# Query stacks loaded in 16 pieces of 512 bytes, from a scratch whose rows have gaps

## What is computed

```
x = x + xattn(layernorm(x), ctx, ctx)         # x, ctx: 128 x 64 x 128
    q = (x @ Wq.T + bq), k = (ctx @ Wk.T + bk), v = (ctx @ Wv.T + bv)   # 16 heads of 8
    scores = q k^T / sqrt(8); attn = softmax(scores); out = (attn v) @ Wo.T + bo
x = x + ffn(layernorm(x))
    so, si = softmax(bottleneck(x))           # two sets of 128 scores a token
    top 32 of so gate (x @ weight), top 32 of si gate x before "@ weight"
    + bias
```

## Time and profile before

| | |
|---|---|
| median of 3 runs | 524.53 us (522.14 to 526.05) |
| the profiled execution, its own time | 522.13 us |
| span of the profiled execution | 520.3 us |
| busy in the span: PE, DVE, ACT, POOL | 414.4, 408.7, 391.4, 363.5 us |
| DMA packets, bytes | 138970, 53.02 MB |
| chain that ended last: SP's queue, DMA | 27%, 7% of the span |
| first phase | to about 290 us |

### The profile page before, as it was taken

How to read it: one execution, slowest core, us unless ns; L and a number is a source line. 1 busy time by engine, 2 the same in 40 slices (tenths; PEclk the granted TensorE clock), 3 DMA queues, 4 the chain that set the end, 5 groups by cost and what they waited for, 6 DMA issues and landing times.

```text
span 520.3 us, 16344 instructions
## 1 busy us (share of the span) xinstructions
PE 414.4 (80%) x5516; PEld 314.0 (60%) x5516; DVE 408.7 (79%) x1940; ACT 391.4 (75%) x1061; POOL 363.5 (70%) x515
## 2 busy tenths in 40 slices
PE   3457999989999989999989564987787877777754
PEld 1125787868877858887777242765564645555543
DVE  7554478766777766767875359999999999999997
ACT  3414677867787858887667488899989898899893
POOL 7356667776777767876311023699989898999896
PEclk9997799988999999999999855578879698788687
DMA  5788788788788787788810000000000000000001
GB/s 159 157 211 196 159 197 196 197 204 195 172 183 184 191 195 176 161 185 182 178 47 7 1 0 2 1 21 23 21 22 37 12 36 22 21 21 22 23 21 40
DMA packets 138970, 53.02 MB, mean 102 GB/s; under 512 B 105146, under 2 KB 131195, under 8 KB 137339
## 3 DMA queue, kind: packets, MB, share of 16 engines
q1 hardware_dynamic: 136712, 51.47, 41.2%
q10 hardware_dynamic: 2176, 0.52, 0.5%
HBM read 34.67 MB, written 16.78 MB: 99 GB/s over the span
## 4 chain that ended last, share of the span: by engine, by line
DVE 37%; SPq 27%; PE 18%; DMA 7%; issue 4%; ACT 4%; POOL 2%; DVEq 0%; ACTq 0%; POOLq 0%
SPq L300 23%; DVE kst L1040 17%; DVE tops L1033 16%; DMA k_scratch<-k_parts 4%; PE ps_pv L360 4%; DMA qst<-q_scratch 3%; PE ps_col L345 2%; SPq L285 2%; PE ps_row L389 2%; PE ps_mix L375 1%; PE ps_proj L437 1%; SPq L247 1%; PE ps_proj L415 1%; PE ps_turn L430 1%; PE ps_mix L604 1%
## 5 line engine op out<-in xcount | busy, mean ns | idle before, releaser
L892 DVE TENSOR_REDUCE m<-ps_row 128x8 f32<-128x512 f32 x128 | 82.3, 686 | 57.1 <-PE ps_row L389 56.9
L650 ACT ACTIVATE pT<-ps_col 128x512 f32<-128x512 f32 x128 | 68.7, 589 | 29.1 <-PE ps_col L345 28.9
L1033 DVE MAX8 tops<-kst 128x8 f32<-128x128 f32 x384 | 78.1, 268 | 0.0
L360 PE MATMUL ps_pv<-vx,pT 128*64 128x18 f32 x2048 | 73.3, 214 | 0.0
L360 PEld LDWEIGHTS ps_pv<-vx,pT 128*64 128x64 f32 x2048 | 66.9, 141 | 7.1 <-issue 4.5
L1040 DVE MATCH_REPLACE8 kst<-tops,kst 128x128 f32<-128x128 f32 x264 | 69.0, 266 | 0.0
L389 PE MATMUL ps_row<-kst,qst 96*64 96x128 bf16 x1024 | 42.7, 228 | 7.8 <-DMA qst<-q_scratch 7.7
L345 PEld LDWEIGHTS ps_col<-qst,kst 100*128 100x128 bf16 x1024 | 35.0, 100 | 22.8 <-issue 11.9
L345 PE MATMUL ps_col<-qst,kst 100*128 100x64 bf16 x1024 | 42.8, 197 | 5.9 <-DMA qst<-mT 5.7
L553 PE MATMUL ps_proj<-wf_sb,x2T 128*128 128x128 f32 x128 | 25.6, 362 | 26.2 <-ACT x2T L821 26.2
L389 PEld LDWEIGHTS ps_row<-kst,qst 96*64 96x64 bf16 x1024 | 33.5, 116 | 11.8 <-DMA qst<-q_scratch 9.9
(11 more groups left out here) (156 smaller groups left out, 1213.3 us busy)
## 6 DMA issues: line engine op xcount, KB each, us to landing
k_scratch<-k_parts SPq DMA_DIRECT2D x32, 192.0 KB, 3.0
q_scratch<-q_parts SPq DMA_DIRECT2D x32, 192.0 KB, 3.1
kst<-k_scratch SPq DMA_DIRECT2D x32, 192.0 KB
qst<-q_scratch SPq DMA_DIRECT2D x32, 192.0 KB
xr<-in_x_dram SPq DMA_DIRECT2D x16, 256.0 KB, 4.3
cT<-in_ctxT_dram SPq DMA_DIRECT2D x16, 256.0 KB, 3.6
kst<-k_scratch SPq DMA_DIRECT2D x32, 128.0 KB
qst<-q_scratch SPq DMA_DIRECT2D x32, 128.0 KB
```

The source lines that it names most:

```text
L360: mm = pe.matmul(pv_flat[pp * SEQ:(pp + 1) * SEQ, h * 2 * VW:(h + 1) * 2 * VW], pT[:, 2 * j + pp, hh, :], vx[s][:, 2 * hp + pp, h, :], sta ...
L650: act.activation(pT[:, b % PT_RING, :, :], ps_col[b % 2][:, :, :], ACT.Exp, scale=SCALE).then_inc(act_exp, 1)
L892: dve.tensor_reduce(m32[:, b // 4, :, 4 * j:4 * j + 4].rearrange("q a h -> q h a"), ps_row[b % 2][:, :, :, :], AX.X, ALU.max).then_inc(dve ...
L1033: ins = dve.max(tops[g % 2][:, n, 8 * rnd:8 * rnd + 8], source(g, rnd, n))
```

## The change

`q_scratch` gets rows of 288 instead of 256 elements (GAP = 32, 64 bytes that nobody reads), so the 16 heads of a row no longer touch: they lie 576 bytes apart. The write to it fills the first 256 of the 288. The queries' stack is read as `(n i) h t`, of which the first 256 elements of `t` are taken, so each row of 8192 bytes in `qst` is filled by 16 pieces of 512 bytes. The number of DMAs, their order, their rows, their bytes, their waits and their semaphores are unchanged, and the keys' scratch and stack keep their shapes (the keys' source is only written in another way). No other engine's program changes.

```diff
+GAP = 32
...
-        q_scratch = [nc.dram_tensor(f"q_scratch{s}", (2, PARTS, 128, HALF), BF16).ap() for s in range(2)]
+        q_scratch = [nc.dram_tensor(f"q_scratch{s}", (2, PARTS, 128, HALF + GAP), BF16).ap() for s in range(2)]
...
                 for a in range(2):
-                    sp.dma_start(scratch[s][a].rearrange("n c t -> c n t"),
+                    sp.dma_start(scratch[s][a, :, :, 0:HALF].rearrange("n c t -> c n t"),
                                  parts[:, :, a * HALF:(a + 1) * HALF]).then_inc(done[s], 16)
...
-                        src = scratch[s][a, first:first + n].rearrange("n (i h) t -> (n i) (h t)", h=HEADS)
+                        src = scratch[s][a, first:first + n].rearrange("n (i h) t -> (n i) h t", h=HEADS)
                         rows = spread(a, n)
                         dst = (kst[d][rows, :, :, a, :].rearrange("r h p m -> r (h p) m") if to_keys
-                               else qst[d][rows, :, :].rearrange("r h t -> r (h t)"))
+                               else qst[d][rows, :, :])
                         if to_keys:
-                            src = src.rearrange("r (x m) -> r x m", m=SEQ)
+                            src = src.rearrange("r h (p m) -> r (h p) m", m=SEQ)
+                        else:
+                            src = src[:, :, 0:HALF]
                         sp.dma_start(dst, src).then_inc(moved[d], 16)
```

## The result

The changed kernel takes 528.68 us in the median of 20 runs (524.9 to 533.4), the kernel before 525.36 us in 20 runs beside it (518.24 to 531.24). The medians differ by 3.3 us (0.6%), the means by 3.7 us (0.7%, with a 95% interval of roughly 2 to 5.5 us). The ratio used from here on, 1.0096 with a 95% interval of 1.0067 to 1.0124 (5.0 us, 3.5 to 6.5), compares only executions within 1.5% of their kernel's fastest, which drops 8 of the 20 of the kernel before, whose fastest is a lone 518.24, and 2 of the 20 changed ones. So the changed kernel is slower, and by 3 to 5 us; these runs don't settle it more closely.

The account below looks back on a forecast made before the run. SP's queue was taken to bound most of the first phase, with PE close behind. Issue time of 3.1 us plus landings of 0.2 us gave 3.3 us, so 527.8 us on a median of 524.53, range 521 to 539 us.

Parts of the forecast that it names:

- Issue time: SP's six queries' stack issues: 45 ns more each, 0.27 us a group, 3.1 us in all.
- The signs that were named: Queries' issues with a minimum near 560 and a median near 665 ns; some 23000 more packets of 512 bytes.
- The upper end of 120 ns: Most that a queries' issue on SP might gain, from the keys' 737 ns against 617; 8.4 us in all.
- 11.6 from the chain: Groups of the 16 in which a longer queries' stack costs time: 120 us on the chain over 10.3 us a group.
- Transfer: Queries' rows on the DMA engines: 0.44 to 0.456 us each, 0.016 more, hidden behind the issue.
- Landing: PE's wait for a group's last queries' transfer: some four landings on the chain at 0.05 us each, 0.2 us.
- Pieces outlast their issue: Above 33 ns a piece, the queries' load sets the pace instead of its issue: 14.7 us more, 539.3 us; chance 0.18.
- Pieces hold up the next issue: SP's issue behind a queries' DMA of 384 pieces is held up: 7 us more, 534.8 us; chance 0.17.
- Smaller packets share better: Shorter packets let `qst<-mT` between them, halving PE's waits: 520.9 us, or 517.8 without the issue surcharge; chance 0.1.
- The rival that the PE slack swallows the change: SP's surcharge is zero or PE's slack takes it, so nothing changes: 524.5 us; chance 0.1.
- a sign of error: The prediction would be wrong if the groups' period were set by PE throughout; no size given.

Follow-up runs that it names:

- wait2: Kernel before, rows whole, with two waits on a long-satisfied semaphore behind each of the queries' six DMAs; ratio 1.0072.
- dst32: Kernel before with the query stack in SBUF broken behind every 128 tokens, so rows come in 32 pieces of 256 bytes; ratio 1.0090, plain medians 1.0200.
- gap256: Changed kernel with a gap of 256 bytes in place of 64, so each piece starts on a 256-byte boundary; ratio 1.0101 to the kernel before.
- dst16: Kernel before, scratch without gaps, with 32 bytes left free behind each head in the query stack in SBUF, 16 pieces a row; ratio 1.0113.
- q5_issue2: Kernel before with the queries' two 8-row DMAs merged into one of 16, plus two small DMAs a group behind them; ratio 0.9987.
- q5: Kernel before with the queries' two 8-row DMAs merged into one of 16, five DMAs in all, rows whole; ratio 0.9921.
- the idle waits: Kernel before with two or five waits on a long-satisfied semaphore behind each of the queries' six DMAs; ratios 1.0072 and 1.0171.

## Why the prediction was right, and where not

**The forecast** was 527.8 us on a median of 524.53, 3.3 us or 0.6% more. Measured were 528.68 on a median of 525.36, again 3.3 us, or 5.0 us (1.0%, 0.67 to 1.24%) by the ratio. The sign and the range hold. The main term, issue time on SP's queue, holds as far as the experiments go. That the medians agree to a tenth of a microsecond is luck: the terms below are off by more than that.

**Issue time.** 40 to 50 ns an issue were read from the keys' issues. The trace has 37 ns more in the minimum and 45 in the median, and 24 to 67 by place in the stack with a mean of 41; the stage grew by 0.24 to 0.25 us where 0.27 were forecast. The signs that were named came out: a minimum near 560 and a median near 665 ns are 555 and 663, and the page has 23040 more packets (162010 for 138970). The upper end of 120 ns rested on one keys' issue of 737 ns, which was the slowest of the 16 at its place; their median is 663. The groups in which it counts were taken as 11.6 from the chain, and the experiments come out at 10 to 12 us per microsecond a group, so the count was sound, though drops of the clock are in it too. This term, forecast at 3.1 us, is then 2.4 to 2.9; wait2, with a third more of SP's time, took 3.8. But it was read from a chain that differs from one execution to the next, 68.8% on SP's stack issues from 60 to 108 us in one and 9.2% in the other, so that so close a count is in part luck.

**Transfer.** A row was to go from 0.44 to 0.456 us and went to 0.51 or 0.53; the step that took the writes' 28.5 ns for the reads was too cheap by 3 to 5 ns a piece. Eight rows in succession were to take 3.65 us against 4.2 of issuing and take 3.8 to 4.2. The load still lies behind its issue, but barely, and dst32 leaves open whether the longer transfer cost nothing, as forecast.

**Landing.** 0.2 us were allowed for the last transfers. PE's wait for the queries' landing grew by 1.9 us in the profiles (9.6 for 7.7), and it was 14.0 and 13.2 us in gap256 and dst16, against 10.1 in wait2. The term is of the right kind and undersized, and what I left out is what follows a longer wait: the clock. In the profiled pair it took some 3 us at one place.

**The sum** of 3.3 us agrees with the medians and is 1.7 below the 5.0 of the ratio, whose interval begins at 3.5. SP's time gives 2.4 to 2.9 us of it. What is left, between 0.4 and 2.6 us, is not assigned by any run: the landing and the transfer are the candidates, and q5_issue2 shows that kernels with equal time on SP's queue can lie 0.9 to 1.1% apart.

**The rivals.** Pieces outlast their issue: not clearly. The prediction put the limit at 33 ns, and the pieces took 29.5 to 33.1; no surcharge like the rival's 14.7 us came out, but a small part of it isn't excluded. Pieces hold up the next issue: no with 384 pieces (556 and 558 ns in the median), a little with the 768 of dst32. Smaller packets share better: no, PE's wait for `qst<-mT` went from 5.7 to 7.2 us, and was 5.7 to 6.8 in the other kernels with pieces. The rival that the PE slack swallows the change fell as well. The prediction named as a sign of error that the groups' period be set by PE throughout; q5 and the idle waits show that it isn't, while the chain of the changed kernel shows that for some stretches it is.

## What to carry to other kernels

Where one queue issues DMAs back to back and the chain runs over it, count issue time before bytes: some 40 ns more on each of six issues a group are worth about 0.5% here by the rate that the idle waits give, more than half of what a form with 16 times the packets a row cost in all by the plain medians. What the bytes and packets themselves cost was too small to tell from nothing. But a queue that gets ahead isn't free either: one issue fewer a group won 0.8%, three fewer lost 4.7%, because the next wait (a small transfer behind the backlog, or the round trip from a write to its reader) was close. Shorten such a queue in steps and look after each at what PE and the queue itself wait for.

## What the runs showed of the hardware

A DMA's issue on SP took 24 to 67 ns more with rows in 16 pieces than with whole rows, and not more with 64 pieces: the issues of 24 rows took 702 to 732 ns whole, 769 in 16 pieces (queries) and 766 to 782 in 64 (keys), those of 8 rows 612 to 618, 659 to 666 and 654 to 663 (medians by place in the stack). A DMA of 4 rows of 8 bytes took SP 467 ns behind the queries' stack, and 295 in the median of three in a row, more than a third of an issue of 24 rows. 8192 bytes in pieces of 512 cost the engines 0.51 to 0.53 us a row against 0.44 to 0.456 in one piece, and the start of a piece on a boundary of 256 bytes changed nothing (32.9 against 33.1 ns). A wait on a semaphore that was long satisfied took SP 26 to 27 ns (0.32 us for 12, 0.79 for 30). And a 16 KB transfer issued by ACT behind 768 KB issued by SP moved no byte for 3.9 us and took 5.7 us from issue to use.
